# A three-stage vision-tower kernel on one core: other PSUM banks for three products, both layer norms applied on ScalarE, small VectorE operations exchanged, first stage reordered

## The reference

```
h = _L0_tok_ref(...)
h = h + _L0_attn_ref(_layernorm(h), wq, wk, wv, wo)
h = h + _L0_ffn_ref(_layernorm(h), W_base, b_base, lora_A, lora_B, router_W, ...)
```

## Time and profile before

| | |
|---|---|
| median of 3 runs | 3473.15 us (3472.47 to 3475.3) |
| profiled execution | 3475.76 us, span 3474.0 us |
| busy, share of the span | PE 85%, DVE 76%, POOL 61%, ACT 51% |
| token stage | 0 to about 363 us |
| weights | to about 440 us |
| tower | to 3474 us |
| chain that ended last | POOL 29%, issue 23%, ACT 14%, PE 10%, DVE 10% |

### The profile page before, as it was taken

The page is one execution under the profiler, slowest core; times in us unless marked ns, Lnnn a source line. Parts: engine busy times, 40 slices in busy tenths (PEclk is TensorE's granted clock), DMA queues, the critical chain, the costliest instruction groups (busy, mean ns, idle before and its releaser), DMA issues.

```text
span 3474.0 us, 61513 instructions
## 1 busy us (share of the span) xinstructions
PE 2937.6 (85%) x16986; PEld 1439.8 (41%) x16986; DVE 2629.2 (76%) x8687; ACT 1756.8 (51%) x5820; POOL 2104.2 (61%) x1610
## 2 busy tenths in 40 slices
PE   1655658999999999999999899999999899999987
PEld 0444523444444444444444444444444444444443
DVE  5999747777777777777777777777777777777773
ACT  1666435555555555555555555555555555555551
POOL 1555036666666666666666666666666666666662
PEclk9777779999999999999999999999999999999998
DMA  6454436666666666666666666666666666666662
GB/s 136 123 139 116 116 82 128 138 129 137 127 134 132 131 132 126 130 133 130 131 133 130 131 127 129 134 129 132 133 131 133 126 131 131 133 128 136 137 125 55
DMA packets 1269006, 442.51 MB, mean 127 GB/s; under 512 B 1200048, under 2 KB 1241264, under 8 KB 1268800
## 3 DMA queue, kind: packets, MB, share of 16 engines
q1 hardware_dynamic: 1235520, 436.42, 60.5%
q10 hardware_dynamic: 33280, 4.20, 1.1%
HBM read 88.15 MB, written 67.11 MB: 45 GB/s over the span
## 4 chain that ended last, share of the span: by engine, by line
POOL 29%; issue 23%; ACT 14%; PE 10%; DVE 10%; DMA 1%; ACTq 1%; POOLq 0%; DVEq 0%; SPq 0%
POOL probs L1004 11%; ACT probs L1080 9%; PE bank_b L1441 8%; POOL p_hl L1008 6%; POOL xy_hl L1018 4%; POOL rope_a L1014 4%; POOL r L1037 4%; DVE share L1208 3%; DVE probs L1199 3%; ACT heads L1109 2%; ACT p_hl L1089 2%; PE bank_a L1441 1%; DVE rsum L1210 1%; ACT at_hi L1095 1%; DVE r L1286 1%
## 5 line engine op out<-in xcount | busy, mean ns | idle before, releaser
L1441 PE MATMUL bank_a<-qkv_hi,xt 128*128 128x512 f16 x3072 | 1002.9, 392 | 183.0 <-DVE v_lo L1241 157.4
L1008 POOL TENSOR_TENSOR p_hl<-probs,p_hl 128x512 f16<-128x512 f32 x512 | 639.0, 1248 | 504.1 <-ACT p_hl L1089 504.1
L1080 ACT ACTIVATE probs<-probs,negmax 128x128 f32<-128x128 f32 x2048 | 790.4, 387 | 255.8 <-DVE negmax L1199 255.5
L1004 POOL TENSOR_TENSOR probs<-probs,rsum 128x512 f32<-128x512 f32 x512 | 566.6, 1107 | 241.1 <-DVE rsum L1210 241.1
L1441 PE MATMUL bank_b<-b_hi,yt 128*128 128x512 f16 x2048 | 642.9, 381 | 0.0
L1199 DVE CUSTOM_DVE_ANT_0 probs<-score,table,scal 128x128 f32<-128x128 f32 x2048 | 595.8, 347 | 57.5 <-issue 57.1
L1089 ACT ACTIVATE p_hl<-probs 128x512 f16<-128x512 f32 x512 | 320.4, 626 | 577.1 <-POOL probs L1004 574.7
L1441 PE MATMUL bank_a<-qkv_lo,xt 128*128 128x512 f16 x1536 | 601.6, 392 | 0.0
L1441 PEld LDWEIGHTS bank_a<-qkv_hi,xt 128*128 128x128 f16 x3072 | 308.0, 100 | 596.5 <-DVE v_lo L1241 158.7
L1109 ACT ACTIVATE heads<-rope_a 128x512 f16<-128x512 f32 x320 | 199.3, 623 | 466.2 <-POOL rope_a L1014 466.2
L1253 DVE TENSOR_TENSOR heads<-rope_a,heads 128x512 f16<-128x512 f32 x320 | 335.9, 1051 | 81.6 <-ACT heads L1109 74.6
(11 more groups left out here) (189 smaller groups left out, 4248.2 us busy)
## 6 DMA issues: line engine op xcount, KB each, us to landing
tok_h<-kout SPq DMA_DIRECT2D x64, 512.0 KB, 6.3
hin<-tok_h SPq DMA_DIRECT2D x64, 512.0 KB, 3.8
r<-tok_h SPq DMA_DIRECT2D x64, 512.0 KB, 3.4
out_dram<-r SPq DMA_DIRECT2D x64, 512.0 KB, 4.1
probs_t<-p_hl SPq DMA_TRANSPOSE x512, 3.2
xc<-in_x_dram SPq DMA_DIRECT2D x32, 128.0 KB, 4.1
raw_a<-in_L_attn_wq_dram SPq DMA_DIRECT2D x1, 4096.0 KB, 14.6
raw_b<-in_L_attn_wo_dram ACTq DMA_DIRECT2D x32, 128.0 KB, 4.3
```

Source lines behind the costliest of these rows:

```text
L1004: TT(x, x, rsum[:, u % 2].unsqueeze(2).to_broadcast([P, GR, T]), ALU.mult).then_inc(s_norm, 1)
L1008: TT(p_hl[:, u % 2, 1], probs[:, u % 2], p_hl[:, u % 2, 0], ALU.subtract).then_inc(s_plo, 1)
L1080: ins = A(probs[:, u % 2, g], probs[:, u % 2, g], ACT.Exp, bias=negmax[:, u % 2, g:g + 1], scale=-1.0, accum_out=sums[:, u % 2, g:g + 1])
L1441: ins = MM(bank, x(c), w[:, c, cols], start=(c == 0 and i == 0), stop=(c == KC - 1 and i == 2))
```

## The change

Token stage: z's second half moves from POOL to DVE, straight out of PSUM, behind the first half; POOL keeps the sum and the swap. ACT's copy of the second transpose goes. The turns are rounded by being written as int32, and one fused operation per row makes the fraction, in place of a rounding and a subtraction over the chunk; the quarter turn comes in as the sine's bias. ACT's copies of chunk ch-1 go with the turn of chunk ch. PE turns x of chunk ch+2 ahead of the products of chunk ch. The 32 loads of wo go to SP, two in each chunk.

Tower: q(1) goes to `bank_c`, the router's product, z's transpose and lora(0) go to `pv`, lora(1) stays in `bank_c` and waits for the rope of q(1) only. Both xyn leave DVE: POOL makes rstd and mean times rstd, and ACT writes the fp16 high part and the fp32 value by two Identity activations. v_low goes ahead of heads_low("k"). L1208 becomes a product of two tensors, and zs[:, 0] is made by products from PSUM in place of a cast.

```
-                nc.gpsimd.tensor_tensor(z2[:, :], by_step(c2[:, :, :]), by_column(L1, nxt), ALU.mult).then_inc(s_z2, 1)
-                nc.gpsimd.tensor_tensor(z[:, nxt], z[:, nxt], z2[:, :], ALU.add).then_inc(s_z, 1)
+                    pool.wait_ge(s_z12, ch + 1)
+                    pool.wait_ge(s_v, ch + 1)
+                    nc.gpsimd.tensor_tensor(z[:, r], z[:, r], z2[:, r], ALU.add).then_inc(s_z, 1)
...
-            for h in range(HQ):
-                at = h // 16 * 512 + h % GR * P + h // GR % 4 * HD
-                act.dma_start(w["raw_b"][:, :, at:at + HD],
...
-                        ins = TS(u[:, nxt, h], const[:, C_L0:C_L0 + L0], tabc[:, nxt, NT - 1, h:h + 1],
+                        ins = TS(k[:, h], const[:, C_L0:C_L0 + L0], tabc[:, nxt, NT - 1, h:h + 1],
                                  const[:, C_Q:C_Q + 1], ALU.mult, ALU.add)
...
-                    TS(k[:, :], u[:, nxt], ROUND, -ROUND, ALU.add, ALU.add).then_inc(s_k, 1)
-                    TT(u[:, nxt], u[:, nxt], k[:, :], ALU.subtract).then_inc(s_f, 1)
+                    for h in range(CH):
+                        ins = STT(u[:, nxt, h], const[:, C_L0:C_L0 + L0], tabc[:, nxt, NT - 1, h:h + 1], k[:, h],
+                                  ALU.mult, ALU.subtract)
...
-                    TT(z[:, nxt], by_step(ct1[:, nxt]), by_column(0, nxt), ALU.mult).then_inc(s_z1, 1)
+                    TT(z[:, nxt], by_step(ct1[:, nxt]), by_column(0, nxt), ALU.mult)
+                    TT(z2[:, nxt], by_step(ct2[:, nxt]), by_column(L1, nxt), ALU.mult).then_inc(s_z12, 1)
```

Tower:

```
+                def scale_shift(mean, var, rstd, shift, done, c):
+                    TT(rstd[:, :], var[:, :], minus_half[:, :], ALU.pow).then_inc(done, 1)
+                    pool.wait_ge(done, c * 2 + 1)
+                    TT(shift[:, :], mean[:, :], rstd[:, :], ALU.mult).then_inc(done, 1)
...
-                    A(xy_hl[:, 0], xyn[:, :], ACT.Copy).then_inc(s_xhi, 1)
+                    A(xy_hl[:, 0], hin[:, :], ACT.Identity, bias=shift1[:, 0:1], scale=rstd1[:, 0:1])
+                    A(xyn[:, :], hin[:, :], ACT.Identity, bias=shift1[:, 0:1], scale=rstd1[:, 0:1]).then_inc(s_xhi, 1)
...
-                    TS(share[:, u % 2], sums[:, u % 2], 2.0 ** -14, None, ALU.mult).then_inc(s_share, 1)
+                    TT(share[:, u % 2], sums[:, u % 2], small[:, :], ALU.mult).then_inc(s_share, 1)
...
-                        src, hs = bank_a[j - 1][:, :], 16
+                        src, hs = (bank_a[0], bank_c)[j - 1][:, :], 16
...
+                    TS(mean[:, :], mv[:, 0:1], -1.0, None, ALU.mult)
...
-                    TS(xyn[:, :], r[:, par], mv2[:, 0:1], rstd2[:, 0:1], ALU.subtract, ALU.mult).then_inc(s_yn, 1)
...
-                    TS(xyn[:, :], hin[:, :], mv1[:, 0:1], rstd1[:, 0:1], ALU.subtract, ALU.mult).then_inc(s_xn, 1)
...
-                    V.tensor_copy(zs[:, 0], zb).then_inc(s_zd, 1)
+                    for i in range(2):
+                        ins = TT(zs[:, 0, i].rearrange("p (a r) -> p a r", r=R), z, weight, ALU.mult)
...
-                        pe.wait_ge(s_rope, n * 3 + 1)
-                        pe.wait_ge(s_vlo, n + 1)
-                    dense(bank_a[j][:, :], xs, "qkv", slice(j * 512, (j + 1) * 512), part, s_q)
+                        await_(pe, s_rope, n * 3)
+                        if finish:
+                            await_(pe, s_lev, f * 2)
+                    dense((bank_a[0], bank_c)[j][:, :], xs, "qkv", slice(j * 512, (j + 1) * 512), part, s_q)
...
-                        pe.wait_ge(s_lev, f * 2 + 1)
-                    MM(bank_c[:, :], zt[:, :], keep["lbs"][:, j * 512:(j + 1) * 512],
+                        pe.wait_ge(s_rope, n * 3 + 3 if qkv else CB * 3)
+                    MM(low_rank[j], zt[:, :], keep["lbs"][:, j * 512:(j + 1) * 512],
```

More of the change, by code:

```diff
@@ L280, in _, with copies @@
                                      .rearrange("p (a b) -> p a b", b=P), ACT.Copy).then_inc(s_tev, 1)
+            def copies(c, h0, h1):
+                for h in range(h0, h1):
+                    act.wait_ge(s_kp, c * CH + h + 1)
+                    if h % 4 == 0 and (not isinstance(c, int) or c >= 1):
+                        act.wait_ge(s_kst[h // 4 % 2], c * 32)
+                    nc.scalar.activation(kout[:, h // 4 % 2, h % 4], kps[h % 4][:, :, :], ACT.Copy).then_inc(s_kev, 1)
             def body(ch, r):
@@ L294, in sine @@
                     act.wait_ge(s_f, ch + 2)
[L295 to L307, removed]
-                if exists(ch + 1):
[L310 to L316, removed]
+                    nc.scalar.activation(u[:, nxt], u[:, nxt], ACT.Sin, bias=qb[:, 0:1], scale=TURN).then_inc(s_sin, 1)
+                if exists(ch - 1):
+                    copies(ch - 1, 0, CH if r else 4)
+                if exists(ch + 1):
+                    (decay if r else sine)(1 - r)
+                if exists(ch - 1) and not r:
+                    copies(ch - 1, 4, CH)
                 if exists(ch + 1):
-                    parts[1](1 - r)
-                if exists(ch):
-                    copies(3, CH)
+                    (sine if r else decay)(1 - r)
             chunks(act, body)
+            copies(NCH - 1, 0, CH)
         @block.vector
@@ L799, in tower @@
         share = sb("share", [P, 2, GR])
+        small = sb("small", [P, GR])
         p_hl = sb("p_hl", [P, 2, 2, GR, T], F16)
@@ L1119, in turn @@
                 if finish:
-                    act.wait_ge(s_yn, f + 1)
+                    act.wait_ge(s_rstd2, f * 2 + 2)
                     act.wait_ge(s_xt, normed(b) * 16)
-                    A(xy_hl[:, 0], xyn[:, :], ACT.Copy).then_inc(s_yhi, 1)
+                    act.wait_ge(s_xlo, normed(b))
+                    A(xy_hl[:, 0], r[:, par], ACT.Identity, bias=shift2[:, 0:1], scale=rstd2[:, 0:1])
+                    A(xyn[:, :], r[:, par], ACT.Identity, bias=shift2[:, 0:1], scale=rstd2[:, 0:1]).then_inc(s_yhi, 1)
                 if attention:
@@ L1164, in turn @@
                     await_(act, s_lo, f * 2)
-                    A(zt[:, :], bank_c[:, 0:P // 2].bitcast(F16), ACT.Copy).then_inc(s_zev, 1)
+                    A(zt[:, :], router[:, 0:P // 2].bitcast(F16), ACT.Copy).then_inc(s_zev, 1)
                 if attention:
@@ L1518, in turn @@
                     pe.wait_ge(s_yt, f * 16 + 16)
+                    if rest:
+                        pe.wait_ge(s_ahi, p * 2 + 2)
+                        pe.wait_ge(s_alo, p * 2 + 2)
                     await_(pe, s_lev, f * 2)
                     for part in range(2):
-                        dense(bank_c[:, 0:AR], ys, "ar", slice(0, AR), part, s_ar)
+                        dense(router[:, 0:AR], ys, "ar", slice(0, AR), part, s_ar)
                     ffn(0, 0)
```

169 lines of the change are left out of this document (87 added, 82 removed).

## The result

The changed kernel takes 3519.81 us (median of 4 runs, 3516.34 to 3521.95) against 3474.23 before, ratio 1.0129 [1.0115, 1.0142]: 46 us slower, about 1.3%. The forecast was 3297. The profiled execution is 3521.95 us long, its span 3520.2.

A forecast was written before the change was run, and what follows sets the result against it. It took DVE, partly stalled by POOL, to bound the token stage, and a softmax chain over DVE, ACT and POOL the tower. 3475.8 - 70 (stage) - 106 (tower) = 3299.8, as a median 3297 us; range 3200 to 3405.

The forecast's parts named there:

- 3.3 us of issue on DVE per pass as before: Tower loop, at the jump to the next pass: DVE's 3.3 us of issue would stay unchanged.
- The router's exponential and high(3) stand behind both writes on ACT, so DVE gets little earlier to its router steps: Tower, second half of a turn, ACT's queue: little gain before DVE's router steps; no size of its own.
- Rival (c): Tower, ACT's queue: four writes for two lengthen the softmax chain; slower, 3544 us at 2.2 us a turn; 6 in 100.
- Its two waits go. In the loop's second turn the chain no longer crosses PE: Tower, PE: waits for v_lo and before lora(1) vanish, saving 1.2 us a pass.
- PE also keeps its clock or loses it in slack: Tower, PE: the clock stays up, or drops only where it costs nothing; no size given.
- for things done microseconds before: Tower, PE: new waits (attend(0), router, kv) are for results finished long before; no cost.
- becomes two products of about 0.2: 0.65 less: Tower, DVE's router steps: the 1.09 us cast of zs replaced by two products, 0.65 us less.
- share: I take no gain: Tower, DVE, L1208 as a product of two SBUF tensors: no gain, as it still contends with POOL.
- Token stage, 70 us less, bounds 35 and 85: First stage: 28 us at the start plus 46 over the chunks, less 4.5 at the end.
- rival (d): Token stage: chunks stay 17 us and more, stage gives 28 - 4.5 + 16 = 40; 3327 us; within the forecast's 60 in 100.
- The tower, 106 us less, bounds 20 and 210: Tower: 3.5 us a pass over 28 passes (98), plus 8 from eight written-out turns at 1.0.
- 0.92 for faster: Whole kernel: probability of a faster time, from the forecast and rivals of 3198 and 3403 us; slower 0.06, same 0.02.

The follow-up runs named there:

- e1: The kernel before with only the change's new first (token) stage, old tower: 3430.79 us, ratio 0.9872.
- e9: The kernel before with 58 one-column DVE memsets ahead of the tower's turns, loop beginning at instruction 962 as in the changed kernel: 3556.57 us, ratio 1.0237.
- e6: The kernel before with the new token stage and 16 DVE memsets, loop beginning at 972: 3311.99 us, ratio 0.9531.
- e7: The kernel before with the new token stage, the new PSUM bank roles, v_low first and 16 DVE memsets: 3324.44 us, ratio 0.9565.
- e14: The kernel before with the new token stage, small DVE operations and both norms on ACT, old banks, loop at 970: 3317.11 us, ratio 0.9548.
- e2: The whole changed kernel with eight one-column DVE memsets ahead of the tower's first turn, loop at 970: 3333.63 us, ratio 0.9594.
- e5: The kernel before with 72 one-column DVE memsets ahead of the tower's turns, loop beginning at 976: 3398.44 us, ratio 0.9783.
- e11: The kernel before with the new token stage, the two small DVE operations (share, zs) and 12 memsets, loop at 972: 3288.42 us, ratio 0.9465.
- e13: The whole changed kernel with eight DVE memsets, and on ACT the router's exponential moved ahead of the first norm's two writes: 3272.32 us, ratio 0.9419.
- e10: The kernel before with 216 DVE memsets ahead of the tower's first turn, loop beginning at 1120: 3464.01 us, ratio 0.997.

## Why the prediction was wrong, point by point

The forecast was 223 us too low. Of these, 128 are the tower's term (106 less forecast, 21.6 more measured without a stand), 110 the place of the loop, and the first stage did 16 better than its term.

- **"3.3 us of issue on DVE per pass as before"** is the step that turned the sign. I saw the issue in the earlier trace rows and took it for a price of the jump. It was the price of a place, and 58 instructions that the change adds on DVE ahead of the loop, 52 of them in the first stage (e1 begins at 956), moved it to where there are two stands. The change of place alone costs 83 us in e9 (3556.6 against 3473.6), and 186.2 - 75.8 = 110 us between the changed kernel and before. Without it the time would have been about 3410, just above my range of 3200 to 3405, and still on the faster side.
- **"The router's exponential and high(3) stand behind both writes on ACT, so DVE gets little earlier to its router steps"**. The place was named, its sign was wrong: DVE gets there later (lrec starts 2.55 us behind the end of lmax on average, 1.20 before), since the exponential had stood behind one Copy of 1.04 and now stands behind two writes at a pitch of 1.14 (1.23 each by their rows, above my 1.04 to 1.16) and POOL's scalars. Putting it first gave 61 us. Rival (c), the longer softmax chain in ACT's queue, had the right queue at 6 in 100, and no price for what follows on PE. That its 3544 lies near the 3519.8 is luck: it stood for 141 us in ACT's queue, where the norms cost 24 to 29.
- **"Its two waits go. In the loop's second turn the chain no longer crosses PE"** with 1.2 us a pass for it, and **"PE also keeps its clock or loses it in slack"** failed. Where there is no stand, PE's idle time in the old tower is spread, 1.4 us for v_lo in one place and 1.3 for the sum in another (e6). The new banks take both away and PE idles in front of zs in their place: 2.7 us a turn in e7, behind which, in about every second turn, 12 matmuls take some 4.2 us for 2.59. e7 differs from e6 in the banks and v_low's order only and is 12.5 us slower. Why is open: the clock (1.00 and 0.98) is what these two traces offer, no run takes it away alone, and from e14 to e2 the banks cost 16.5 us with the clock at 0.98 in both. The new waits "for things done microseconds before" were indeed small: none of them is among PE's longer waits in e2. A pass without a stand takes 89.8 us in e5 and 90.3 in e2, where 3.5 less had been forecast.
- The cast that **"becomes two products of about 0.2: 0.65 less"** gave 0.23. The products take 180 ns, as said, but the stall went on to the subtraction behind them. The gain of e11, 23.6 us, is all the same more than this step alone.
- **"share: I take no gain"** was right (374 to 366 ns), and the rule behind it fits the rows.
- **Token stage, 70 us less, bounds 35 and 85**: it is worth 86, just outside, and the stage by itself ends 95.7 us earlier (360.9 to 265.2). The start came at 26.7 us as said, 27.6 of the 28 us; most chunks take 13.6 to 14.1 us and not 15, because the product's loop at slow clock, which I had put next, doesn't hold DVE up in most chunks: 59 us in place of 46. The end, from the last table copy to the last copy out of PSUM, got 9 us shorter (41.9 to 32.5) where I had added 4.5. In e1 43 us of it were hidden by the second stand, and for that run rival (d), "the stage does not shorten", would have looked true.
- **The tower, 106 us less, bounds 20 and 210**: with no stand it is 21.6 us more (e6 to e2), outside the bounds. With the exponential first it is 39.7 us less (e6 to e13), inside them. The written-out turns, forecast 42.4, take 44.6 to 45.5 in the changed kernel and 43.9 to 44.0 in e13.
- The 0.92 for faster (its parts, 60, 18 and 15 in 100, make 0.93) had every rival but two on the faster side. None of the cases was one in which the change leaves the work as it is and moves code.

## What to carry to other kernels

When a trace shows an engine standing some 3 us in front of an instruction that waits for nothing, at every jump of a loop, look at the packets of the instruction queue and at the loop's place before pricing anything else; here the packets were the same with one stand and with two. A loop like this one, of 374 to 378 instructions, runs clean or with one or two stands depending only on where it begins, so compare variants with the same number of blocks touched, or an added instruction will be read as the cost of an edit.

When a small result with a long chain behind it shares a queue with large writes, give it the place ahead of them: that was worth 61 us here. And idle time of PE can cost more than its length once it is gathered in one place (in e7 2.7 us, and in about every second turn some 1.6 more in the matmuls behind it).

## What the runs showed of the hardware that I had not expected

- A stand of 3.5 us at each jump of a loop that touches three blocks of instructions, and a second of 2.2, 2.5 or 3.1 us at a start 11, 9 or 5 instructions ahead of the next block. A pass of 90 us becomes 2.3 to 2.8 us longer with the first (e10 and before, against e5) and 4.5 to 7.0 with both (e1 against e6, the changed kernel against e2).
- Idle time of PE split in two main places (1.4 and 1.3 us a turn, e6) left the granted clock at 1.00 over the middle of the tower; about the same time in one place (2.7 us, e7) brought it to 0.98, with the lower level behind some of the waits and not behind others of the same length.
